# ScalarE writes the mask into the score bank for blocks 0, 3 and 6 of every eight (before: 2 and 6) in a masked cross attention

## The reference

```python
energy = jnp.einsum('nqhd,nkhd->nhqk', q, k)             # 16 heads of 32 columns, 512 queries, 8192 keys
energy = jnp.where(mask == 0, jnp.float32(-1e+20), energy)
attention = jax.nn.softmax(energy / jnp.sqrt(jnp.float32(EMBED)), axis=3)
out = jnp.einsum('nhql,nlhd->nqhd', attention, v).reshape(n, q_len, EMBED)
return out @ Wo.T + bo
```

## Time and profile before

| | |
|---|---|
| median of 3 runs | 4119.28 us (4115.73 to 4119.32) |
| the profiled execution: its own time | 4116.4 us |
| its span, first to last instruction | 4114.7 us |
| first masked cross attention, loop over the pairs | about 425 to 1430 us of the span |
| busy in these 1005 us: PE, DVE, ACT, POOL | 988.76, 723.39, 728.30, 807.60 us |
| granted TensorE clock in them | 1.00 of full speed |

### The profile page before, as it was taken

How to read it: one execution, slowest core, us unless ns; L and a number is a source line. 1 busy time by engine, 2 the same in 40 slices (tenths; PEclk the granted TensorE clock), 3 DMA queues, 4 the chain that set the end, 5 groups by cost and what they waited for, 6 DMA issues and landing times. The chain is left out here.

```text
span 4114.7 us, 51578 instructions
## 1 busy us (share of the span) xinstructions
PE 3793.2 (92%) x17986; PEld 2235.4 (54%) x17986; DVE 2806.0 (68%) x3506; ACT 2342.5 (57%) x3656; POOL 1865.1 (45%) x1116
## 2 busy tenths in 40 slices
PE   7999999999999975789999899999999988769998
PEld 6887444444444342257888644444444345448886
DVE  4333877777777269946888777777777353568888
ACT  2223777777777734423777446666666620437775
POOL 1001587887887719910000348888888800000001
PEclk9999999999999987989999989999999997789999
DMA  8997566666676521023888767777777521218887
GB/s 308 333 341 256 136 155 153 154 155 156 150 158 151 121 81 58 0 96 129 318 320 321 256 175 174 178 172 175 171 170 170 120 71 53 62 72 320 323 317 267
DMA packets 295660, 750.48 MB, mean 182 GB/s; under 512 B 55630, under 2 KB 89166, under 8 KB 260842
## 3 DMA queue, kind: packets, MB, share of 16 engines
q1 hardware_dynamic: 246522, 570.48, 41.8%
q0 software_dynamic: 48880, 176.71, 21.5%
HBM read 475.44 MB, written 98.96 MB: 140 GB/s over the span
## 5 line engine op out<-in xcount | busy, mean ns | idle before, releaser
L993 ACT ACTIVATE prob<-psum 128x512 f32<-128x512 f32 x1628 | 918.2, 598 | 398.7 <-PE psum L869 365.8
L1185 POOL TENSOR_TENSOR den_pool<-den_pool,prob 128x1024 f32<-128x1024 f32 x405 | 1020.3, 2519 | 79.4 <-DVE den_pool L1094 33.0
L869 PE MATMUL psum<-q_stack,k_ring 98*128 98x512 f32 x2048 | 959.1, 499 | 20.5 <-ACT prob L993 16.9
L1065 DVE CUSTOM_DVE_ANT_0 psum<-psum,mask_q 128x1024 f32<-128x1024 f32 x512 | 627.0, 1235 | 225.0 <-PE psum L831 207.2
L1061 DVE TENSOR_REDUCE row_max<-psum 128x1 f32<-128x1024 f32 x512 | 610.0, 1220 | 222.0 <-PE psum L831 216.6
L869 PEld LDWEIGHTS psum<-q_stack,k_ring 98*128 98x128 f32 x2048 | 394.5, 193 | 524.7 <-ACT psum L999 199.3
L831 PE MATMUL psum<-k_ring,q_stack 96*128 96x512 f32 x2048 | 667.9, 408 | 7.5 <-DVE row_max L1061 4.5
L1945 DVE TENSOR_TENSOR weight_lo<-weight_raw,weight_hi 128x2048 fp32r<-128x2048 f32 x180 | 411.4, 2290 | 113.8 <-ACT weight_hi L1941 113.6
L880 PE MATMUL psum<-prob,x 128*32 128x512 f32 x3256 | 473.4, 606 | 3.1 <-ACT prob L993 0.8
L831 PEld LDWEIGHTS psum<-k_ring,q_stack 96*128 96x128 f32 x2048 | 388.2, 193 | 93.5 <-issue 18.2
L2120 POOL DMA_DIRECT2D y_slots<-xnT x28 | 15.4, 549 | 862.5 <-ACT xnT L2224 862.5
(11 more groups left out here) (463 smaller groups left out, 6608.6 us busy)
## 6 DMA issues: line engine op xcount, KB each, us to landing
den_dma<-prob POOLq DMA_DIRECT2D x211, 512.0 KB, 5.0
k_ring<-k_hi SPq DMA_DIRECT2D x1024, 64.0 KB, 2.3
weight_raw<-in_L_ffn_Wu SPq DMA_DIRECT2D x60, 1024.0 KB, 7.0
weight_raw<-in_L_ffn_Wd SPq DMA_DIRECT2D x60, 1024.0 KB, 5.1
weight_raw<-in_L_ffn_w SPq DMA_DIRECT2D x60, 1024.0 KB, 6.8
den_dma<-xnT POOLq DMA_DIRECT2D x72, 512.0 KB, 5.0
k_ring<-k_lo SPq DMA_DIRECT2D x512, 64.0 KB, 2.6
w_o<-in_L_ffn_w SPq DMA_DIRECT2D x30, 1024.0 KB, 7.2
```

Source lines behind the costliest of these rows:

```text
L869: e.matmul(out, k_ring[:, n % kring, kt * P:(kt + 1) * P], q_stack[h % n_q][:], start=not masked, stop=True, skip_group_check=masked and b ...
L993: e.activation(prob[b // 2 % n_p][:, b % 2, :], bank_of("block", b), ACT.Exp, scale=scale).then_inc(s_exp, 1)
L1065: e.tensor_tensor_reduce(out=max_banks(q), in0=max_banks(q), in1=masks[0][:, i, 2 * c2 * KC:2 * (c2 + 1) * KC], scale=1.0, scalar=-3.0e38, ...
L1185: e.tensor_tensor(den[:], den[:], tile, ALU.add).then_inc(s_dpool, 1)
```

## The change

A tuple `MASK_FIRST = (0, 3, 6)` names the blocks of every eight whose mask ScalarE writes; `by_scalar(b)` asks for it and `masks_done(b)` counts which mask write a block waits for. On TensorE these blocks wait for `s_pre` and leave out the mask matmul. On ScalarE the write for block b is issued right after the exponential of block b-2, which for block 3 of eight is behind the second exponential of a pair; that of block 0 of the whole stage is issued ahead of the loop. Blocks 0 and 3 of eight go from TensorE to ScalarE, block 2 goes from ScalarE to TensorE, block 6 stays where it was.

```diff
+MASK_FIRST = (0, 3, 6)
+def by_scalar(b):
+    return b % 8 in MASK_FIRST
+def masks_done(b):
+    return len(MASK_FIRST) * (b // 8) + MASK_FIRST.index(b % 8) + 1
...
-                if masked and b % 4 == 2:
-                    e.wait_ge(s_pre, b // 4 + 1)
+                if masked and by_scalar(b):
+                    e.wait_ge(s_pre, masks_done(b))
                 else:
                     wait_for_bank(e, "block", b)
-                if masked and b % 4 != 2:
+                if masked and not by_scalar(b):
                     e.matmul(out, k.ident_big[:], masks[1][:, t, :], start=True, stop=False)
...
             m_hi_rows(0)
+            if masked:
+                mask_first(0)
             for g in range(H * PAIRS):
                 h, p = divmod(g, PAIRS)
                 exponentials(2 * g)
-                if masked and g % 2 == 0:
+                if masked and by_scalar(2 * g + 2) and 2 * g + 2 < H * KT:
                     mask_first(2 * g + 2)
...
                 exponentials(2 * g + 1)
+                if masked and by_scalar(2 * g + 3) and 2 * g + 3 < H * KT:
+                    mask_first(2 * g + 3)
```

More of the change, by code:

```diff
@@ L862, in scores @@
                 out = bank_of("block", b)
-                if masked and b % 4 == 2:
-                    e.wait_ge(s_pre, b // 4 + 1)
+                if masked and by_scalar(b):
+                    e.wait_ge(s_pre, masks_done(b))
                 else:
                     wait_for_bank(e, "block", b)
-                if masked and b % 4 != 2:
+                if masked and not by_scalar(b):
                     e.matmul(out, k.ident_big[:], masks[1][:, t, :], start=True, stop=False)
                 e.matmul(out, k_ring[:, n % kring, kt * P:(kt + 1) * P], q_stack[h % n_q][:],
-                         start=not masked, stop=True, skip_group_check=masked and b % 4 == 2).then_inc(s_score, 1)
+                         start=not masked, stop=True, skip_group_check=masked and by_scalar(b)).then_inc(s_score, 1)
             def wave(h, w):
```

## The result

The changed kernel takes 4146.14 us (median of 4 runs, 4145.67 to 4147.95) where the kernel before takes 4118.25 us (4 runs, 4115.73 to 4119.32): a ratio of 1.007, 95% interval 1.0058 to 1.0083, 28 us slower. The forecast was 4148 us.

What follows compares the result with a forecast made beforehand. TensorE's matmul stream was taken as the bound; +38.1 (block 0), +3.5 (block 40) and -11.5 (blocks 2 and 3) made +30 us on 4116.4, or 4146.5, put at 4148 us (+0.7%), range 4126 to 4166.

Steps and rivals of the forecast that it cites:

- The bound, and the wait that was none: Masked loop: TensorE's matmul stream bounds; the 199.3 us named as waiting for ScalarE's mask write before L869 is no wait.
- Blocks 2 and 3, 0.09 us: Masked loop: block 3 saves 0.23 us, block 2 costs 0.14 more; together 0.09 us saved per eight blocks, -11.5 us.
- The chain at block 0, 0.30 us: Block 0 waits for its mask write behind block 6's exponential; TensorE 0.30 us later per eight blocks, 127 times, +38.1 us.
- Block 40: Once a head its write must await block 38's exponential in the same bank: 0.53 us, 0.23 extra, 15 heads, +3.5 us.
- Nothing catches this up, since TensorE had no slack: Masked loop: the 0.30 us lost at block 0 per eight blocks is not regained later.
- the sum of 30: Masked loop total: +38.1 for block 0, +3.5 for block 40, -11.5 for blocks 2 and 3, together +30 us.
- That the weights of the waiting block load early: Rival for block 0: weights load ahead of the wait, mask load behind the wave is free; +3 us, 4121; chance 0.08.
- That the time is given back behind the wait: Rival: block 0's wait replaces later ScalarE waits, so all saved matmul time counts; -29 us, 4089 us; chance 0.07.
- That block 3 waits too: Rival: block 3 also waits on ScalarE, a further 0.3 us in 128 places; +68 us, 4186 us; chance 0.06.
- what the profile was to show: Signs included the loop 30 us longer, eight blocks in 7.70 us, PE's busy time some 10 to 60 us less.
- The other four at 72 to 80%: Reading of the masked attention's loop: the four engines besides PE are busy for 72 to 80% of its 1005 us.

Runs made afterwards that it cites:

- the run with blocks 3 and 6: Changed kernel with block 0 of eight given back to TensorE, so ScalarE writes only the masks of blocks 3 and 6: 4105.75 us, ratio 0.9977.
- two writes in the bad places: Changed kernel with ScalarE writing the masks of blocks 0 and 4 of eight instead of 0, 3 and 6: 4217.77 us, ratio 1.0245.
- four, only one of them badly placed: Changed kernel with ScalarE writing the masks of blocks 2, 3, 6 and 7 of eight instead of 0, 3 and 6: 4092.46 us, ratio 0.9948.

## Why the prediction was right, and what of it was off

**The bound, and the wait that was none.** Right. TensorE's stream is the pace, and the 0.84 us in front of L869, 199.3 us by name, bought nothing when the mask write was moved away from it: behind the wave the idle time stayed 0.84 us and took another name.

**Blocks 2 and 3, 0.09 us.** Right. From block 1 to block 4 of eight the median over the stage fell from 2.81 to 2.73 us (0.08), and the run with blocks 3 and 6, which has this part alone, gained 10 us where 11.5 were expected.

**The chain at block 0, 0.30 us.** Right, piece by piece: forecast +0.54, +1.03, +1.64, +1.69, +2.03, measured +0.54, +1.03, +1.63, +1.68, +2.02. From block 6 to the start of block 9 of eight the median went from 2.20 to 2.49 us, +0.29.

**Block 40.** Right: in the changed kernel the maxima step behind it is 2.98 us from block 38's load, before 1036.97 - 1034.51 = 2.46, +0.52 against the 0.53 forecast:

```profile
1051.08 0.19 PEld L880 LDWEIGHTS psum<-q_stack,k_ring 98*128 98x128 f32 x1 [0.84 <-issue]
...
1053.06 0.60 ACT L1010 ACTIVATE psum<-mask_k 128x512 f32<-128x512 fp8e4 x1
...
1053.71 0.19 PEld L880 LDWEIGHTS psum<-q_stack,k_ring 98*128 98x128 f32 x1 [1.61 <-ACT psum L1010]
...
1054.06 0.64 PE L842 MATMUL psum<-k_ring,q_stack 96*128 96x512 f32 x2
```

**"Nothing catches this up, since TensorE had no slack".** Wrong once a head, and it is the 2 us by which the sum of 30 was too large. In blocks 16 to 23 the kernel before took 7.64 us in place of 7.49, because pair 8's maxima step waited for VectorE. In a head of the kernel before, with 0.23 us for a matmul, its load would stand at 1012.29 + 0.23 = 1012.52; it starts at 1012.78, 0.12 behind the end of the reduction of pair 6, and the row says issue:

```profile
1012.29 0.10 PEld L868 LDWEIGHTS psum<-mask_k,ident_big 128*128 128x128 bf16 x1 [0.25 <-ACT prob L993]
...
1012.52 0.14 DVE L1065 DVE_READ_ACCUMULATOR2_ANT row_max<- 128x1 f32 x1
...
1012.78 0.30 PEld L831 LDWEIGHTS psum<-k_ring,q_stack 96*128 96x128 f32 x2 [0.28 <-issue]
```

The changed kernel reaches that place later, by 0.2 us for each group of eight, and no longer waits: 7.71 us, +0.07 where the other groups have +0.21. That is 0.14 x 15 = 2.1 us. (The last head has no such maxima step. There the sum fits by luck, +1.6 us against +1.35 measured: its first four groups of eight blocks lose 0.8 us each, and blocks 32 to 47 win back 2.0, because the kernel before waits for accumulating DMAs there, with ScalarE idle for 1.85 and 1.59 us, while the changed one has none.) I had looked at VectorE's share of the whole loop, 72%, and not at the four pairs in which it has the adds to do.

**The rivals.** That the weights of the waiting block load early: the load at 1036.50 starts 0.05 us behind the write's end at 1036.45, so not here. That the time is given back behind the wait: no, the 0.29 us stay. That block 3 waits too: its weight load stands 0.50 us behind its write's end in the median, and 0.05 us behind it only 8 times of 128, seven of them in the last head. Of what the profile was to show, one number came out low: PE's busy time fell by 6.4 us over the kernel and by 9.6 in the loop (979.20 us between 425 and 1460, from 988.76), not by 10 or more. Records of waiting matmuls reach into the wait: the rows show 50.8 / 127 = 0.40 us of idle array, the starts 0.54.

**A misread row.** "The other four at 72 to 80%" holds for three engines; the weight loads, PEld, are busy for 426.64 of 1005 us, 42%. Nothing in the sum uses it.

## What to carry to other kernels

Where work is handed from the engine that bounds to one that is idle for a quarter of the time, ask for each instance what lies between the result it hangs on and the point where it is wanted, and write it down in starts: here 1.69 us of chain were free where a wave of 1.00 us lay in between and cost 0.3 us where none did, and two writes in the bad places cost 100 us while four, only one of them badly placed and that once a head, gained 25. Do it for the exceptions too: where a bank is lent out, the chain is longer and the helping engine's order is another. Look for an earlier slot in the helping engine's order before giving an instance up. And before counting on a gain per group, find the stretch in which the second busiest engine is packed: its share of the whole loop does not show it.

## What the runs showed of the hardware that I had not expected

A VectorE addition of two SBUF tiles, issued while a GpSimd addition was running, ended 1.09 us behind the GpSimd one's end and took 2.51 us, twice its 1.22; with none running it took 1.22. Over all 14 traces 80 of these additions were issued more than 0.16 us before the end of a GpSimd addition. They took 1.27 to 3.42 us, and every one ended 1.08 or 1.09 us behind the GpSimd one's end, so the addition stood still rather than ran slower; the 771 that met no GpSimd addition took 1.21 to 1.23 us. It holds the other way round as well: 15 GpSimd additions issued while one of VectorE's ran took 3.18 to 3.38 us in place of 2.52 and ended 2.22 to 2.25 us behind VectorE's. The Trainium skill, "SBUF — State Buffer", under "Who interferes with whom", says that a VectorE instruction with two SBUF inputs contends with a GpSimd instruction that reads SBUF, and that the later one blocks fully; these rows agree, and VectorE's reductions of PSUM against one SBUF tile kept their 1.23 us under the same GpSimd adds (the row at 872.96; 1.20 to 1.27 us for all 2643 that ran wholly under one), as the page has it for one SBUF input.
